# A graph kernel's accumulation banks handed out anew: one for segment sums, three for counted pairs, four for sums, and a new pace for late node chunks

## The reference

```python
h = gelu(x @ W_pre + b_pre)
aggr = segment_sum(h[src] * edge_attr, dst)         # layer 0
x1 = x + aggr
y = gelu(gelu(x1 @ W1 + b1) @ W2 + b2)
x = layernorm(x + x1 + y)
deg = segment_sum(1, dst); dinv = rsqrt(maximum(deg, 1))
h = x @ W_lin.T + b_lin                             # layer 1
agg = segment_sum(h[src] * (dinv[src] * dinv[dst])[:, None], dst)
out = layernorm(x + relu(agg + x @ W_root.T + b_root))
```

## Time and profile before

| | us |
|---|---|
| median of 3 runs | 1655.67 |
| lowest, highest | 1640.36, 1659.41 |
| the profiled execution | 1638.62 |
| its span | 1636.8 |

### The profile page before, as it was taken

How to read it: one execution, slowest core, us unless ns; L and a number is a source line. 1 busy time by engine, 2 the same in 40 slices (tenths; PEclk the granted TensorE clock), 3 DMA queues, 4 the chain that set the end, 5 groups by cost and what they waited for, 6 DMA issues and landing times.

```text
span 1636.8 us, 21570 instructions
## 1 busy us (share of the span) xinstructions
PE 1092.7 (67%) x7839; PEld 911.3 (56%) x7839; DVE 720.9 (44%) x1396; ACT 504.6 (31%) x825; POOL 827.7 (51%) x927
## 2 busy tenths in 40 slices
PE   3274455655555766766668877787876388839897
PEld 2263233333334645655567675677766287738797
DVE  7028455655464465363445545432214133333435
ACT  0121345455453454343345345330000000000105
POOL 7457656655555455454445544454555545554003
PEclk9977767768778768887988988888888598958999
DMA  6432455545455465564666666675656266626653
GB/s 151 113 99 60 147 166 179 180 150 163 134 183 158 128 220 176 173 218 122 199 196 217 201 208 196 191 234 148 198 166 167 62 179 161 190 61 179 161 131 77
DMA packets 192321, 263.64 MB, mean 161 GB/s; under 512 B 70450, under 2 KB 169778, under 8 KB 185234
## 3 DMA queue, kind: packets, MB, share of 16 engines
q1 hardware_dynamic: 164528, 218.27, 43.1%
q0 software_dynamic: 27392, 43.48, 11.3%
q10 hardware_dynamic: 290, 0.45, 0.1%
HBM read 175.09 MB, written 87.00 MB: 160 GB/s over the span
## 4 chain that ended last, share of the span: by engine, by line
PE 48%; another core or an unknown queue 23%; ACT 14%; issue 10%; DVE 4%; DMA 0%; DVEq 0%; SPq 0%; ACTq 0%
PE bank_q L1437 23%; ACT counts_raw L915 12%; PE seg L1377 10%; PE bank_q L1408 9%; PE bank_a L1337 1%; PE bank_q L1509 1%; DVE onehot L1190 1%; DVE hots_raw L1283 1%; PE bank_q L1337 1%; DVE msg L1206 1%; PE seg L1509 0%; PE bank_b L1469 0%; PE bank_b L1337 0%; PE bank_q L1489 0%
## 5 line engine op out<-in xcount | busy, mean ns | idle before, releaser
L829 POOL DMA_INDIRECT gath<-table_h,srcs x791 | 764.4, 966 | 677.5 <-DVE msg L1206 456.6
L915 ACT CAST counts_raw<-bank_q 128x490 bf16<-128x490 f32 x625 | 403.3, 696 | 504.0 <-remote 244.6
L1437 PE MATMUL bank_q<-piece_raw,early_late 128*96 128x240 bf16 (+1 forms) x3735 | 476.0, 283 | 55.5 <-issue 53.0
L1437 PEld LDWEIGHTS bank_q<-piece_raw,early_late 128*96 128x96 bf16 x3735 | 429.5, 134 | 85.9 <-issue 78.8
L1408 PE MATMUL bank_q<-hots_raw 128*128 128x245 bf16 x1250 | 268.0, 313 | 302.1 <-ACT counts_raw L915 230.2
L1408 PEld LDWEIGHTS bank_q<-hots_raw 128*128 128x128 bf16 x1250 | 102.8, 106 | 427.1 <-ACT counts_raw L915 286.8
L1377 PE MATMUL seg<-onehot,msg 128*97 128x128 f32 x1662 | 286.0, 331 | 68.7 <-issue 47.4
L1377 PEld LDWEIGHTS seg<-onehot,msg 128*97 128x97 f32 x1662 | 258.3, 211 | 81.1 <-issue 58.0
L1281 DVE TENSOR_TENSOR hots_raw<-counters,kb 128x1024 bf16<-128x1024 bf16 (+1 forms) x157 | 107.2, 683 | 214.7 <-PE bank_q L1408 160.3
L1283 DVE TENSOR_TENSOR hots_raw<-counters,kb 128x1960 bf16<-128x1960 bf16 (+1 forms) x157 | 182.5, 1163 | 0.0
L1303 DVE TENSOR_TENSOR sumT<-sumT,bank_q 96x240 f32<-96x240 f32 x91 | 36.4, 400 | 249.9 <-remote 132.3
(11 more groups left out here) (170 smaller groups left out, 584.9 us busy)
## 6 DMA issues: line engine op xcount, KB each, us to landing
counts_hbm<-counts_raw SPq DMA_DIRECT2D x53, 1470.0 KB
piece_raw<-counts_hbm SPq DMA_DIRECT2D x260, 240.0 KB
edg<-in_edge SPq DMA_DIRECT2D x166, 240.0 KB
gath<-table_h,srcs POOLq DMA_INDIRECT x791
piece_raw<-counts_hbm SPq DMA_DIRECT2D x50, 120.0 KB
piece_raw<-counts_hbm SPq DMA_DIRECT2D x26, 180.0 KB
counts_raw<-counts_hbm SPq DMA_DIRECT2D x4, 600.0 KB, 6.8
table_h<-stage SPq DMA_DIRECT2D x12, 192.0 KB
```

Source lines behind the costliest of these rows:

```text
L829: pool.indirect_dma_start(gath[0:k, u % GS * UT + j, :], None, table[0], bass.IndirectOffsetOnAxis(ap=srcs[0:k, t:t + 1], axis=0)).then_in ...
L915: act.copy(counts[:, k % 2, :, i * 2 * WD:(i + 1) * 2 * WD].rearrange("p a (w n) -> p w a n", w=2), bank_q[m % 2][:, 0:2 * KC].rearrange(" ...
L1437: mm = pe.matmul(sums(r)[0:D, 0:n], parts[:, FINE[c] + i, part, :], rows, start=(first and runs[r][3] is None and i == 0 and part == 0), s ...
```

## The change

One bank `seg` instead of two; a group's first product now waits for the add of the group before. The segment products are an item "seg" of their own in the order, in the middle of the unit's slots, and at their start in the last 12 units and the tail. The freed bank is `bank_q3`. Pairs take banks 0, 1 and 3 in turn and wait for the cast three before. Runs after the counting take four banks in turn. There, a dense add is written two units after its run's end instead of one (until four units before the end), and up to three runs instead of two may stand waiting when another begins. `RATE` is 1 for chunks 0 to 6, then 2, 2, 3, 3, 4, 6 for chunks 7 to 12. The credit after the counting is 13 instead of 16 tiles, and the least gain there 4 instead of 8. `LATER` has the same value as before in both its places. Left out below are the same renaming of `seg` in a path that these inputs don't take.

```diff
--- before.py
+++ after.py
@@ -52,8 +52,9 @@
 PHASES = (12, 8)
-RATE = (1, 2, 4, 6)
-LATER = 1
+
+RATE, RATE_LAST = 1, (2, 2, 3, 3, 4, 6)
+LATER = (1, 1)
 ZS = 4
@@ -78,8 +79,8 @@
 BUILD_STEP = 0.65
-CREDIT = (11.0, 16.0)
-LEAST = (8, 2)
+CREDIT = (11.0, 13.0)
+LEAST = (8, 4, 2)
@@ -141,12 +142,12 @@
     order, pieces, runs = [], [], []
-    added = [min(last_unit(g) + LATER, ALL_UNITS) for g in range(GROUPS)]
+    added = [min(last_unit(g) + LATER[g >= WIDE], ALL_UNITS) for g in range(GROUPS)]
     steps = {u: [] for u in range(ALL_UNITS)}
...
         at = max(at, added[needed(c) - 1] + 1)
-        rate = RATE[(c >= CUTS - 5) + (c >= CUTS - 3) + (c >= CUTS - 2)]
+        rate = RATE if c < CUTS - 7 else RATE_LAST[c - (CUTS - 7)]
         for p in range(PHASES[0]):
@@ -187,14 +188,15 @@
     def flush(u):
-        while waiting and waiting[0][0] < u:
+
+        while waiting and waiting[0][0] < u - (u > built + 1 and u < UNITS - 4):
             order.append(("dense", waiting.pop(0)[1]))
...
             if e is not None:
-                while len(waiting) > 2:
+                while len(waiting) > 3:
                     order.append(("dense", waiting.pop(0)[1]))
@@ -219,6 +221,8 @@
         for i in range(slots):
+            if i == (slots // 2 if u < UNITS - 12 else 0):
+                order.append(("seg", u))
             for k, (p, c) in enumerate(steps[u]):
@@ -231,7 +235,7 @@
                 if open_run or not (waiting and u <= built + 1):
-                    next_piece(u, LEAST[u > ALL_UNITS - 12])
+                    next_piece(u, LEAST[(u > built + 1) + (u > ALL_UNITS - 12)])
                 if len(pieces) > was:
@@ -387,10 +391,10 @@
-        seg = [bank(f"seg{q}", [P, 512]) for q in range(2)]
+        seg = bank("seg", [P, 512])
         bank_a, bank_b = (bank(f"bank_{q}", [P, 512]) for q in "ab")
...
-        bank_q = [bank(f"bank_q{q}", [P, 512]) for q in range(3)]
+        bank_q = [bank(f"bank_q{q}", [P, 512]) for q in range(4)]
         counters = bank("counters", [P, 512])
@@ -512,7 +516,10 @@
         def bank_of(r):
-            return 2 if r < one_bank else (r - one_bank) % 3
+            return 2 if r < one_bank else (r - one_bank) % 4
+
+        def pair_bank(m):
+            return bank_q[(0, 1, 3)[m % 3]]
@@ -594,7 +601,7 @@
         def set_bank(c):
-            return (bank_q[0], bank_q[1], bank_q[2], seg[0], seg[1], bank_a, bank_b)[c % 7]
+            return (bank_q[0], bank_q[1], bank_q[2], bank_q[3], seg, bank_a, bank_b)[c % 7]
@@ -913,7 +920,7 @@
                 act.copy(counts[:, k % 2, :, i * 2 * WD:(i + 1) * 2 * WD].rearrange("p a (w n) -> p w a n", w=2),
-                         bank_q[m % 2][:, 0:2 * KC].rearrange("p (w a n) -> p w a n", w=2, n=WD)
+                         pair_bank(m)[:, 0:2 * KC].rearrange("p (w a n) -> p w a n", w=2, n=WD)
                          ).then_inc(s_kept, 1)
@@ -1222,7 +1229,7 @@
                 dve.tensor_tensor(sumT[:, bass.ds(b, WIN)], sumT[:, bass.ds(b, WIN)],
-                                  seg[g % 2][0:D + 1, 0:WIN], ALU.add).then_inc(s_add, 1)
+                                  seg[0:D + 1, 0:WIN], ALU.add).then_inc(s_add, 1)
@@ -1370,11 +1377,11 @@
                 pe.wait_ge(s_msg, u + 1)
-                if u == first_unit(g) and g >= 2:
-                    pe.wait_ge(s_add, g - 1)
+                if u == first_unit(g) and g >= 1:
+                    pe.wait_ge(s_add, g)
                 n = len(sizes(u))
                 for j, k in enumerate(sizes(u)):
-                    last = pe.matmul(seg[g % 2][0:D + 1, 0:WIN], msg[0:k, u % MS, j, :], onehot[0:k, u % MS, j, :],
+                    last = pe.matmul(seg[0:D + 1, 0:WIN], msg[0:k, u % MS, j, :], onehot[0:k, u % MS, j, :],
                                      start=(u == first_unit(g) and j == 0),
@@ -1402,10 +1409,10 @@
                     pe.wait_ge(s_kb, m + 1)
-                else:
-                    pe.wait_ge(s_kept, m - 1)
+                elif m >= 3:
+                    pe.wait_ge(s_kept, m - 2)
                 for w in range(2):
-                    last = pe.matmul(bank_q[m % 2][:, w * KC:(w + 1) * KC], hot_b(j)[:, i, :, w], hot_k(j)[:, i, :, w],
+                    last = pe.matmul(pair_bank(m)[:, w * KC:(w + 1) * KC], hot_b(j)[:, i, :, w], hot_k(j)[:, i, :, w],
                                      start=True, stop=True)
@@ -1481,7 +1488,7 @@
                     pe.wait_ge(s_base, n // FINALS * CUTS + CUTS)
-                elif c >= 3 and n < FINALS:
+                elif c == 4 and n < FINALS:
                     pe.wait_ge(s_add, GROUPS)
@@ -1524,7 +1531,7 @@
                 what = item[0]
-                if what == "unit":
+                if what == "seg":
                     unit(item[1])
```

More of the change, by code:

```diff
@@ L1017, in general_unit @@
                                       sumT[0:rows, bass.ds(w * WIN, WIN)],
-                                      seg[0][0:rows, 0:WIN], ALU.add).then_inc(s_ladd[r], 1)
+                                      seg[0:rows, 0:WIN], ALU.add).then_inc(s_ladd[r], 1)
             with dve.Fori(0, UNITS) as g:
@@ L1555, in general_unit @@
                                 values = msg[0:k, 0, j, 0:rows] if r == 0 else gath[0:k, j, 0:rows]
-                                last = pe.matmul(seg[0][0:rows, 0:WIN], values, onehot[0:k, 0, j, :],
+                                last = pe.matmul(seg[0:rows, 0:WIN], values, onehot[0:k, 0, j, :],
                                                  start=(j == 0), stop=(j == tiles - 1))
```

## The result

The changed kernel takes 1704.16 us (median of four runs, 1702.38 to 1712.9) against 1657.54 (1640.36 to 1662.04) beside it: ratio 1.035, 95% interval 1.029 to 1.042 (the medians differ by 47 us, the ratio is 59 us on 1657). Forecast were 1594 us, and 1548 to 1660. The time lies outside the range, on the other side.

A forecast was written before the change was run, and what follows sets the result against it. TensorE was taken as busiest, yet only 67% of the span, idling for lack of pieces and during unbroken gathers. -37 + 4 + 3 - 32 = -62 us gave 1576.6, plus 17.1 to the median: 1594 us, range 1548 to 1660.

The forecast's parts named there:

- So nothing there: Segment products moved mid-unit: VectorE's later add is covered by 9.1 us of TensorE work against 0.8 to 2; no cost.
- Thin stretches: 1255 to 1310 and 1422 to 1468 us, units without pieces: filling them wins 37 us, bounds 0 and 60.
- price per gather: TensorE's idle time per gather after the counting stage: 0.908 us where work is thin to fall to 0.345.
- full stretches: 1080 to 1255 and 1310 to 1422 us: 0.345 us idle per gather, claimed to become the stage's price everywhere.
- Third bank: Pairs in the counting stage: evens out TensorE's and ScalarE's waits, -32 us, bounds 0 and 126.
- single bank: Segment sums: next group's first product waits for an add in the last 12 units, +4 us, bounds 0 and 17.
- The slower rival: VectorE runs further ahead, rows of gathers lengthen, TensorE stands still longer: 1730 us; chance 0.12.
- The rival after the Trainium skill: After 1080 us, units without pieces merely lack work, so all 60 us idle return: 1571 us; chance 0.12.

The follow-up runs named there:

- Frozen: Condition of ten runs, unchanged kernel before at 1648 to 1675 us: TensorE nearly stands still late in a row of gathers.
- plan-only kernel: Kernel before with only new chunk pace, credit, least gains and dense adds a unit later: 1668.45 us, 1.016 frozen; 1158.31 us, 0.985 free.
- before, again: Kernel before, unchanged, run and profiled once more on a later chip, frozen: 1664.45 us.
- change, products first: Changed kernel with segment products back at the unit's beginning on TensorE: 1672.9 us, 0.997 frozen; 1160.83 us, 0.987 free.
- repeats, products first: Changed kernel, segment products at the unit's beginning, TensorE held up by repeated products in every fourth unit: 1846.88 us, frozen.
- repeats, the change: Changed kernel, segment products in the middle, TensorE held up by repeated products in every fourth unit: 1896.12 us, frozen.
- rows of fifteen: Kernel before with GpSimd waiting for messages only every third unit, so at least fifteen gathers in a row: 1868.09 us, 1.119 frozen; 1180.0 us, 1.000 free.
- experiment 3: TensorE held up by repeated products every fourth unit, frozen: kernel before 1839.72 us, change 1896.12, change with segment products first 1846.88; unchanged before 1664.45.
- coupled change: Changed kernel, gathers also waiting for TensorE's segment products of eight units before: 1487.71 us, 0.903 frozen; 1174.33 us, 0.995 free.
- Free: Condition of eight runs, kernel before at 1176 or 1180 us: TensorE never nearly stands still late in a row of gathers.
- banks alone: Changed kernel with the old plan and segment products at the unit's beginning: 1177.7 us, 1.001 free; not run frozen.
- coupled kernel before: Kernel before, gathers also waiting for TensorE's segment products of eight units before: 1560.38 us, 0.933 frozen; 1180.04 us, 1.000 free.

## Why the prediction was wrong

*Sum and parts.* The forecast was -62 us. Frozen, on 1657 us: plan +26 (1.0155), banks -30 (0.9973 less 1.0155; the two intervals together give or take 18; the third run in waiting, which the plan-only kernel leaves out, is in this), middle place +63 (1.0354 less 0.9973; give or take 14). That is +59. Each ratio is to before beside it, on three occasions.

*By stage*, from the first and last cast of a pair in each profile. These are single executions, and before by itself differs by 30 us in the counting:

| frozen, us | until the first cast | counting | behind it |
|---|---|---|---|
| before, in the record | 158.1 | 928.5 | 550.2 |
| before, again | 160.0 | 958.7 | 544.0 |
| plan alone | 157.8 | 948.7 | 549.9 |
| change, products first | 157.4 | 928.7 | 566.7 |
| change | 169.5 | 964.0 | 569.0 |
| repeats, products first | 186.0 | 1003.6 | 657.7 |
| repeats, the change | 183.5 | 1055.1 | 657.3 |

In both pairs the middle place costs its time while pairs are counted (35 and 52 us) and hardly any behind it (2 and 0 us); in the plain pair another 12 us stand ahead of the first cast. The burst shown above is from behind it: it shows how a row comes about, not where the 63 us lie.

*The step that failed: "The segment products moved ... The cover is a unit of TensorE's work, 9.1 us ... So nothing there".* It priced the add's wait against VectorE's slack and asked who stands behind it on VectorE. It did name the order (masks, messages), but the add waits up to 29.4 us, which that cover doesn't hide: TensorE waited 106.5 us for the masks behind it, up to 9.3 us at a time. And it didn't ask what three messages at once do on the next engine: they open three units of gathers together, and rows of fifteen are what cost 12% by themselves. Measured in place of nothing: 63 us, and 49 in the pair of experiment 3. That the place of the products costs this is shown; how it divides between masks and rows is not.

*Thin stretches, -37 us.* That they would fill was right, and the plan and the windows show it (units 128 to 134 and 148 to 152 were empty, one more each than the prediction says). The price per gather was the wrong step: "the full stretches are what the stage becomes everywhere". The plan alone has, from 1100 to 1596 us,

```profile
1100.00:1596.00 496.00, 383.47 (x2877) 344.04 (x2878) 156.90 (x397) 30.44 (x48) 230.55 (x238) 0.81 0.57 157
```

(496 - 383.47) / 238 = 0.473 us a gather. Before it was (476 - 350.86) / 240 = 0.521 over the whole stage, and the forecast's stage, 439 us with 350.86 busy, had 0.367. The prediction read that the price hangs on the length of the row, and then took the full stretches' price for the whole stage. But filling the units didn't shorten the rows: in the plan-only kernel GpSimd pauses 77 times, before 82 and 86. What the plan does move is 16 pieces from behind the gathers to between them: behind the last gather 117.3 us are left instead of 129.0 and 131.0, and from the last cast to the last gather it takes 432.6 us instead of 421.2 and 412.9. So behind the counting the plan is worth about nothing (table). The +26 us (10 to 41 by the interval) aren't found there either, and up to unit 108 the two kernels have the same order, item by item: where they come from stays open. The price forecast is reached only by the coupled change, from 995 to 1433 us:

```profile
995.00:1433.00 438.00, 355.63 (x2851) 327.93 (x2850) 155.47 (x396) 30.39 (x48) 240.96 (x246) 0.86 0.64 177
```

(438 - 355.63) / 246 = 0.335 us.

*Third bank, -32, single bank, +4.* Together -28, measured about -30, with bounds of -12 and -48. TensorE's wait for casts, 203.0 us with products first, moved as forecast: 27 us less than in the record, 64 less than in before on the same chip (267.4). The single bank shows as 16.8 us, in 9 waits, in which segment products wait for an add; that was forecast as 4 us with a bound of 17. Free, the banks are worth nothing, though the wait for casts falls there too, to 48.6 us with the banks alone against 74.1 in before with rows of fifteen: the gathers set the pace there.

*The slower rival* had a part of the mechanism: segment sums that bind VectorE only each third unit, rows longer, TensorE frozen longer. It gave 1730 us and 0.12; the time was 1704. Late masks were not in it. What the prediction held against it, that each run's dense add still waits for TensorE, didn't prevent it: in the burst above two dense adds (L1310) stand between the three messages, and neither waits. The argument of this rival and that of "nothing there" contradict each other; the prediction let both stand, and gave the sum to the second.

*The rival after the Trainium skill* ("SBUF — State Buffer", section "Who interferes with whom": TensorE and ScalarE never wait on anyone). Free, the trace agrees: 318.42 busy us of 400 beside unbroken gathers. Frozen, TensorE nearly stands still, 5.18 us of 13.5; since the profile doesn't name what it waits for, this doesn't show that a port is what it waits for.

*How much the rows explain.* From 9.2 to 15.8 gathers in a mean row (before, rows of fifteen) the time rises by 193 us, 29 us a gather. Between products first (10.4) and the change (11.0) that gives 18 us of 63. The mean is too coarse, for TensorE slows only late in a row. Over all rows of the change behind 160 us it is busy 0.86 to 0.91 of the time during the first five gathers, 0.78 in the sixth, 0.61 in the seventh, 0.41 in the eighth and 0.30 to 0.42 from the ninth to the fourteenth, whatever it waits for. Counting the gathers past the eighth of each row, there are 267 in before and 423 with rows of fifteen, so 1.24 us each; products first has 287 and the change 328. The 41 between them would be worth 51 us of the 63. That is an estimate from single profiles, and it fails elsewhere: the pair with repeats has 256 and 267, which would give 14 us of its 49, and the coupled kernel before has 233, which would give 42 of the 115 us that it wins. So the rows can be a large part in the plain pair, but they don't explain the other two. What makes the frozen condition is open, and so is whether a late TensorE alone, free, makes the middle place costly: experiment 3 fell into the other condition.

## What to carry to other kernels

When an instruction moves later on one engine, follow its semaphore past the engine that waits: if that engine then lets several things go at once, ask what the next engine does with the bunch. Ask too what stands behind the waiting instruction on its own queue, here the masks. Gathers in longer rows cost 12% here, and a wait that is only added, tying the issuer to the engine that consumes, won 7%, both in one condition only. Measure a change on more than one chip and at more than one time before giving it a sign: this one is 3.5% slower in one condition and 1% faster in the other.

## What the runs showed of the hardware

The kernel before took 1176.41 us and, on the same chip later, 1675.09 us, a factor of 1.42. Gathers, casts and masks were as long in one condition as in the other (gathers 969 ns frozen, 985 free). TensorE made the difference: it was busy 1082.5 us for 965.1, with a granted clock of 0.819 for 0.906, and idle 580 us for 211 (before, frozen, and before with rows of fifteen, free). It slowed from about the sixth gather of an unbroken row; in the burst above one to four matmuls came at a time, with gathers 1.25 us apart. From 300 to 700 us the granted clock of the changed kernel was 0.72 for 0.93, so more of it at the 1.2 GHz level, where TensorE was busy 228.48 us for 318.42. Nothing in the profile names what it waited for.
